# A GpSimd outer product for the second half of the first scan step, and a new VectorE order around it, in the last chunk of a two-layer transformer kernel

## What is computed

```python
def step(S, kvq):
    k_t, v_t, q_t = kvq
    k_norm = k_t / (jnp.linalg.norm(k_t, axis=-1, keepdims=True) + 1e-06)
    retrieved = jnp.einsum('bnij,bnj->bni', S, k_norm)
    delta = v_t - retrieved
    S_new = jnp.tanh(S + jnp.einsum('bni,bnj->bnij', delta, k_norm))
    Sq = jnp.einsum('bnij,bnj->bni', S_new, q_t).reshape(B_, n)
    out = Sq * jax.nn.silu(Sq)
    return (S_new, out)
```

## Time and profile before

| | |
|---|---|
| median of 3 runs | 1147.56 us (1147.47 to 1148.2) |
| the profiled execution's own time | 1148.24 us |
| its span, first to last instruction | 1146.3 us |
| TensorE busy | 1096.8 us, 96% |
| VectorE busy | 954.2 us, 83% |
| ScalarE busy | 596.7 us, 52% |
| GpSimd busy | 516.8 us, 45% |
| mean granted TensorE clock | 0.983 of full speed |

### The profile page before, as it was taken

The page is one execution under the profiler, slowest core; times in us unless marked ns, Lnnn a source line. Parts: engine busy times, 40 slices in busy tenths (PEclk is TensorE's granted clock), DMA queues, the critical chain, the costliest instruction groups (busy, mean ns, idle before and its releaser), DMA issues.

```text
span 1146.3 us, 16623 instructions
## 1 busy us (share of the span) xinstructions
PE 1096.8 (96%) x5837; PEld 850.3 (74%) x5837; DVE 954.2 (83%) x1382; ACT 596.7 (52%) x1009; POOL 516.8 (45%) x426
## 2 busy tenths in 40 slices
PE   9999999999999999999999999999999999998386
PEld 5566666678787777788778887877887787886165
DVE  4798888882045998999899899989989998999886
ACT  2345555554446346645755574565557455644534
POOL 1477666774333244433424432443343344337852
PEclk9999999999999999999999999999999999999679
DMA  7246555523532430523134133314232330430001
GB/s 265 102 167 236 211 204 209 222 93 114 179 94 58 145 110 21 146 74 129 56 110 138 46 110 91 128 39 126 77 124 73 110 128 19 129 92 20 0 1 39
DMA packets 45114, 127.01 MB, mean 111 GB/s; under 512 B 4352, under 2 KB 21504, under 8 KB 43136
## 3 DMA queue, kind: packets, MB, share of 16 engines
q1 hardware_dynamic: 43904, 114.20, 31.5%
q10 hardware_dynamic: 1152, 12.07, 2.8%
HBM read 117.86 MB, written 19.92 MB: 120 GB/s over the span
## 4 chain that ended last, share of the span: by engine, by line
PE 77%; DVE 12%; POOL 6%; issue 3%; ACT 2%; POOLq 0%; DVEq 0%; ACTq 0%
PE lower L1257 46%; PE bank L1257 18%; PE lower L440 5%; PE lower L572 2%; POOL state L748 2%; POOL rgn L757 2%; PE bank L1246 1%; DVE y L847 1%; DVE y L852 1%; PE bank L487 1%; POOL a_lo L2017 1%; DVE tmp L2265 1%; PE lower L526 1%; PE lower L530 1%; PE bank L440 1%
## 5 line engine op out<-in xcount | busy, mean ns | idle before, releaser
L2017 POOL TENSOR_TENSOR a_lo<-whole,a_hi 128x512 fp32r<-128x512 f32 x128 | 181.9, 1438 | 267.0 <-ACT a_hi L1629 195.7
L1257 PE MATMUL lower<-b_hi,ring 128*128 128x512 f32 x512 | 193.6, 396 | 1.4 <-ACT a_hi L1629 1.4
L1257 PE MATMUL lower<-b_lo,ring 128*128 128x512 f32 x512 | 190.6, 390 | 1.7 <-POOL b_lo L2017 1.7
L1257 PE MATMUL lower<-a_hi,ring 128*128 128x512 f32 x496 | 186.3, 394 | 1.7 <-issue 1.7
L1257 PE MATMUL lower<-a_lo,ring 128*128 128x512 f32 x496 | 184.1, 389 | 0.3 <-POOL a_lo L2017 0.3
L2017 POOL TENSOR_TENSOR b_lo<-whole,b_hi 128x512 fp32r<-128x512 f32 x64 | 93.5, 1469 | 145.4 <-ACT b_hi L1629 145.4
L1612 ACT ACTIVATE S<-S 128x1024 f32<-128x1024 f32 x56 | 58.6, 1058 | 173.5 <-DVE S L2278 173.5
L1628 ACT ACTIVATE whole<-lower,hs 128x512 f32<-128x512 f32 x126 | 86.2, 685 | 79.3 <-PE lower L1257 77.3
L1257 PEld LDWEIGHTS lower<-b_hi,ring 128*128 128x128 f32 x512 | 96.2, 188 | 22.0 <-issue 1.8
L1257 PEld LDWEIGHTS lower<-b_lo,ring 128*128 128x128 f32 x512 | 96.0, 188 | 22.0 <-POOL b_lo L2017 2.3
L440 PE MATMUL lower<-wa,xT 128*128 128x512 f32 x240 | 109.5, 599 | 1.5 <-DVE turned L817 1.4
(11 more groups left out here) (302 smaller groups left out, 2398.9 us busy)
## 6 DMA issues: line engine op xcount, KB each, us to landing
ring<-ffn_copy_dram SPq DMA_DIRECT2D x128, 512.0 KB, 3.6
look<-ffn_dram ACTq DMA_DIRECT2D x6, 1879.0 KB, 6.9
ffn_copy_dram<-ffn_dram SPq DMA_DIRECT2D x4, 2112.0 KB, 11.4
rope<-rope_dram SPq DMA_DIRECT2D x8, 512.0 KB, 8.2
xtok<-x_dram SPq DMA_DIRECT2D x8, 512.0 KB, 4.2
x1in<-x_dram SPq DMA_DIRECT2D x8, 512.0 KB, 4.8
x1res<-x_dram SPq DMA_DIRECT2D x8, 512.0 KB, 3.3
xT<-xT_dram SPq DMA_DIRECT2D x7, 512.0 KB, 8.4
```

The lines of the kernel that those rows point to most:

```text
L1257: ins = nc.tensor.matmul(out, a, b, start=(first and n == 0), stop=(last and n == len(pairs) - 1))
L2017: nc.gpsimd.tensor_tensor(lo[:, m, :], t["whole"][:, m % 4, :], hi[:, m, :].bitcast(F32), ALU.subtract).then_inc(lo_done, 1)
```

## The change

Half 1 of step 0 is done by `state_delta(0)`, `outer_product(0)` and `state_added(0)` in place of `next_state(0, 1)`. On VectorE `scaled_keys(2, ...)` stands between the first and the last of them, and `read_sums(0)` moves from ahead of `next_state(1, 0)` to behind it. On GpSimd `outer_product(0)` goes ahead of `read_q(0, 0)`. The counts of the semaphores follow.

```diff
-            READS = {(0, 0): 1, (0, 1): 2, (1, 0): 3, (1, 1): 4, (2, 0): 6, (2, 1): 7, (3, 0): 9}
-            OUTERS = {1: 5, 2: 8}
-            TIMES_K = {(0, 0): 1, (0, 1): 2, (1, 0): 3, (1, 1): 4, (2, 0): 6, (2, 1): 7}
-            DELTAS = {1: 5, 2: 8}
+            READS = {(0, 0): 2, (0, 1): 3, (1, 0): 4, (1, 1): 5, (2, 0): 7, (2, 1): 8, (3, 0): 10}
+            OUTERS = {0: 1, 1: 6, 2: 9}
+            TIMES_K = {(0, 0): 1, (0, 1): 2, (1, 0): 4, (1, 1): 5, (2, 0): 7, (2, 1): 8}
+            DELTAS = {0: 3, 1: 6, 2: 9}
...
                         pool.wait_ge(fin_times_k, DELTAS[s])
-                        if s == 2:
+                        if s:
                             pool.wait_ge(fin_pre, 2 * s + 2)
...
                     added_root(0, every, t["rstd4"], t["shift4"])
+                    outer_product(0)
                     read_q(0, 0)
                     read_q(0, 1)
...
                         dve.wait_ge(fin_times_k, TIMES_K[s, 1])
-                        if s == 2:
-                            dve.wait_ge(fin_readq, OUTERS[1])
+                        if s:
+                            dve.wait_ge(fin_readq, OUTERS[s - 1])
...
                     next_state(0, 0)
-                    next_state(0, 1)
+                    state_delta(0)
                     scaled_keys(2, slice(2, BATCH))
+                    state_added(0)
+                    next_state(1, 0)
                     read_sums(0)
-                    next_state(1, 0)
                     state_delta(1)
                     read_sums(1)
                     state_added(1)
```

## The result

| | before | after |
|---|---|---|
| median of the runs | 1147.69 us (6 runs, 1147.28 to 1148.2) | 1152.09 us (6 runs, 1152.02 to 1152.24) |
| ratio, 95% interval | 1 | 1.0039 (1.0029 to 1.005) |
| span of the profiled execution | 1146.3 us | 1150.3 us |
| the profiled execution's own time | 1148.24 us | 1152.07 us |

What follows compares the result with a forecast made beforehand. VectorE's queue in the last chunk's scan was taken to bound the kernel; new port waits, less the removed outer product, made +4.65 us: 1148.24 + 4.65 = 1152.89, less 0.68, gives 1152.2 us, range 1149.2 to 1155.4.

Steps and rivals of the forecast that it cites:

- The bound: Last chunk's scan: VectorE's queue between 1079.43 and 1111 sets the end, microsecond for microsecond.
- GpSimd and VectorE take turns: VectorE instructions with two SBUF inputs and GpSimd's SBUF reads alternate, each shut out for the other's whole instruction.
- sharing: Rival: VectorE and GpSimd each wait for half of the other; +1.6 us, 1149.2; chance 0.03.
- no mutual waiting: Rival: only GpSimd's queue from outer_product(0) to outer_product(1) counts; +0.8 us, 1148.4, no change; chance 0.05.
- Worse turns: Rival: GpSimd takes two turns at state_delta(1), or a lower clock behind it; +6.2 to +7.8, 1153.8 to 1155.4; chance 0.10.
- Two holds at step 1: state_delta(1) on VectorE: product 2.50 us for 1.87 (+0.63), held by read_q(1, 0); difference +0.82, held by read_q(1, 1).
- The sum: Delay of mixed_pair(0, 0) and all behind it: 4.65 us.
- The forecast's own spread: Likeliest case 1152.2, spread 1151.0 to 1153.7: one meeting more or less by 0.8, clock -0.6 to +1.2; chance 0.77.
- the ledger: VectorE's gains and losses: outer product -1.27, difference -0.1, keys +0.36, addition +2.16, product +2.05, state_delta(1) +0.63 and +0.82; together +4.64.
- The keys beside the outer product: VectorE's key scaling waits for GpSimd's new outer product and ends at 1084.83: 2.09 us for 1.73, +0.36.
- The off-load rule: Rival from its first half: only the removed outer product counts, -1.27, 1146.3, chance 0.02; by its warning no gain.

Runs made afterwards that it cites:

- e5: The kernel before with the keys scaled behind the product of next_state(0, 1), ahead of GpSimd's reads: 1146.77 us, ratio 0.9989.
- e10: As the kernel before with the keys scaled ahead of GpSimd's reads, plus the two products of a step back to back ahead of them: 1144.85 us, ratio 0.9976.
- e3: The changed kernel with GpSimd's two reads of step 0 replaced by memsets: one run, 1149.45 us.
- e4: The changed kernel with the first operand of step 0's second-half addition taken from PSUM instead of SBUF: 1151.28 us, ratio 1.0031.
- e2: The kernel before with only read_sums(0) moved behind next_state(1, 0), no new outer product on GpSimd: 1148.96 us, ratio 1.001.
- e1: The changed kernel with read_sums(0) back ahead of next_state(1, 0), the outer product still on GpSimd: 1150.12 us, ratio 1.0019.
- e9: The changed kernel with the keys scaled inside state_delta(0), before the new outer product: 1153.1 us, ratio 1.0044.
- e6: On top of e5, mixed_pair(0, 0) ahead of state_delta(2) and added_root(1) ahead of read_q(3, 0): 1148.92 us, ratio 1.0009.
- e7: As e6, with mix_gates(1, 1) on ScalarE also ahead of add_rows(1) and add_squares(1): 1147.56 us, ratio 0.9997.

## Why the prediction was right, step by step

- **The bound.** The forecast said that VectorE's queue up to L2553 sets the end. After, TensorE is still released by it, 4.72 us later. e5 and e10 show the same from the other side: what goes from that queue comes off the end. The last stretch of the way is not quite the one forecast: the chain after has GpSimd's last read and roots and ScalarE's rows in place of TensorE's gates, but both ways hang on the same queue of VectorE.
- **GpSimd and VectorE take turns.** The forecast ends were 1084.83, 1087.05, 1088.14, 1090.36 and 1091.45; the trace after has 1084.88, 1087.08, 1088.16, 1090.37 and 1091.45 on a clock that is 0.06 later. e3 shows that it takes GpSimd's reads and not just a busy GpSimd, e4 that it takes a second SBUF operand of VectorE. The rivals of sharing and of no mutual waiting fall with the 3.25 and 3.23 us. Worse turns fall too: at step 1 the product ends 1.09 us after the first of the two reads (1100.30 against 1099.21), not after both.
- **Two holds at step 1.** Forecast: product 2.5, difference near 1.1; measured 2.56 and 1.07. Its cause, the third read behind the first sum, is shown alone in e2 (2.56 and 1.06).
- **The sum.** Forecast +4.65 at `mixed_pair(0, 0)`, measured 4.73 with 0.06 of origin: 4.67. e1 splits it: 2.2 from the outer product on GpSimd, 2.4 with the place of the sums. e2 has 1.5 for the sums alone, so the two parts make 0.9 more together than apart. The traces show where. In e1 the first sum runs beside the second read without being held, and from it to the product pass 3.47 us for 2.26 us of sums: 1.2 lost. In the changed kernel the product stands at that place and is held: 3.23 us for 1.22, 2.0 lost.
- **What was a little off.** The end: on the profiled executions the forecast was 1152.89, and 1152.07 was measured. TensorE's gates ran at the upper clock level, which the forecast had named and bounded at 0.6 us of gain; it was 0.7 at the transposes. The link that bounded the transposes was `mix_gates(1, 1)` on ScalarE first, with the rows of x3, which I had named, right behind (their last row ended at 1126.06, the transposes began at 1126.18), and it is over these rows that the chain of the end goes. The median came out at 1152.1 beside the forecast 1152.2, since the profiled execution before lay 0.55 above its median and the one after on it; that closeness is in part luck.
- **Slips in the working, none of which carries the result.** The row of 6.60 us in the earlier trace rows was taken for sixteen matmuls at the lower clock level, but the granted clock was back at 1.00 in 1094.80 to 1095.00, and the row ends at 1095.51; so the price of a low clock was set too small. The forecast's own spread of 1151.0 to 1153.7 isn't the sum of its parts, which give 1150.8 to 1154.2, and the terms of the ledger add up to 4.65, not 4.64.
- **The keys beside the outer product** I had booked as +0.36. e9 shows that the place is good within the change: with the keys elsewhere the product ends 0.75 us later in the trace, and the median is 1 us higher (the intervals of the two ratios overlap).
- **The off-load rule.** The Trainium skill (Perfetto Trace Analysis, "Optimizing Scalar/DVE Operations") warns that moving work between these two engines might not help. The runs agree: in e1, which is the off-load without the moved sums, 1.27 us off VectorE's queue came back as 3.5 us of holds and waiting (2.24 and 1.27). e10 shows the other half of it, that work already on GpSimd is paid for by where VectorE's two-input instructions stand.

## What to carry to other kernels

Before work goes from VectorE to GpSimd, list VectorE's instructions that have two SBUF inputs in the stretch where GpSimd will read large tiles, and add the whole remaining GpSimd instruction to each that falls into it; put sums and one-input or PSUM-operand instructions there, and the two-input ones together ahead of the reads (e10: -3.05 us with no work removed). When a consumer is moved, look at what its semaphore frees: the moved sums cost 1.5 us at a place five instructions away, through a read that reuses their buffer. And an instruction that seems only to wait in the queue may be the cover of another engine's work (e6, e7).

## What the runs showed of the hardware that I had not expected

Who gets the next turn is decided by who stands in the queue at that moment, to within 0.1 us. In e9 VectorE's addition was released by the outer product's own semaphore 0.08 us after GpSimd's next read had started (1085.83 against 1085.75), and was held for all of that read: 3.35 us. In the changed kernel the keys had been issued during the outer product, and went in between it and the read that started at 1084.29.

The granted clock of TensorE decided 1.7 us of a stretch: the same sixteen gate matmuls took 3.72 us in the changed kernel, e2, e3, e4, e5, e9 and e10, and 5.41 in the kernel before and in e1. The idle time ahead of them doesn't tell which: it was 2.07 us both in e5 (3.72) and in the kernel before (5.41). No run settles it. In every kernel with 3.72, TensorE then stood idle for 0.73 or 0.74 us for ScalarE's tanh, so that the clock's gain never came through whole.
